# Moving the tensor engine's wait for the score banks, in the slot that carries the feed-forward part, from the first key to the first up-projection

## What is computed

```python
x = x + block(layernorm(x), cond, ctx)      # h1 = adaln(x); x += mha(h1, h1)
                                            # h2 = adaln(x); x += mha(h2, context)
                                            # h3 = adaln(x); x += glu_ff(h3)
x = x + moe(layernorm(x))                   # 8 experts, 2 of them per token
# mha: 16 heads of 64; scores / sqrt(64); softmax; weighted values; output projection
# glu_ff: u = x @ w1 + b1; (a * gelu(gate)) @ w2 + b2, width 512
```

## Time and profile before

| | |
|---|---|
| median of three runs | 2303.79 us |
| lowest, highest | 2301.26, 2304.38 us |
| the profiled execution | 2302.38 us |
| its span in the trace | 2300.6 us |
| tensor engine busy | 2129.9 us (93%) |
| vector, scalar, GpSimd engine busy | 1265.9, 1282.2, 821.0 us |
| mean granted clock of the tensor engine | 0.972 of 2.4 GHz |

### The profile page before, as it was taken

One profiled execution on the slowest core, in us unless ns is written; L12 is line 12 of the kernel. 1 busy time (PEld: TensorE's weight loads), 2 busy tenths in 40 slices (PEclk: granted clock), 3 DMA queues, 4 the chain that ended last, 5 costly groups with the idle time before them and its releaser, 6 DMA issues. The chain is left out here.

```text
span 2300.6 us, 36836 instructions
## 1 busy us (share of the span) xinstructions
PE 2129.9 (93%) x10284; PEld 1293.0 (56%) x10285; DVE 1265.9 (55%) x3230; ACT 1282.2 (56%) x2450; POOL 821.0 (36%) x1022
## 2 busy tenths in 40 slices
PE   4899999999999999999999999999998777799996
PEld 4455555555555555555555555555555455577774
DVE  3454656565656666565656565656454434245454
ACT  3565666665666666656666666666556433344432
POOL 1132223334242424233333333332423333355553
PEclk8999999999999999999999999999999978999998
DMA  4001111111121111111211111111122111122264
GB/s 141 24 24 42 46 32 47 47 47 50 41 56 41 47 51 41 46 52 40 55 42 46 42 46 42 50 42 46 51 61 84 47 38 39 33 57 57 59 216 151
DMA packets 134421, 127.63 MB, mean 55 GB/s; under 512 B 14649, under 2 KB 108377, under 8 KB 134298
## 3 DMA queue, kind: packets, MB, share of 16 engines
q1 hardware_dynamic: 125018, 108.03, 16.9%
q0 software_dynamic: 9280, 18.28, 2.4%
HBM read 86.63 MB, written 40.67 MB: 55 GB/s over the span
## 5 line engine op out<-in xcount | busy, mean ns | idle before, releaser
L1651 POOL TENSOR_TENSOR pr<-pr,sm 128x512 f32<-128x512 f32 x256 | 262.7, 1045 | 760.4 <-DVE sm L1255 760.4
L706 PE MATMUL ps<-tt,V 128*128 128x512 f32 x1024 | 501.7, 594 | 4.5 <-ACT tt L981 4.5
L981 ACT ACTIVATE kp<-ps 128x512 f32<-128x512 f32 x512 | 295.8, 600 | 198.7 <-PE ps L269 195.3
L1245 DVE TENSOR_REDUCE mx<-ps 128x8 f32<-128x512 f32 x256 | 176.7, 690 | 335.5 <-PE ps L663 332.3
L663 PE MATMUL ps<-kp,hf 128*64 128x256 f32 x2048 | 279.2, 395 | 11.6 <-DVE pr L1248 8.7
L269 PE MATMUL ps<-hk,M 128*128 128x512 f32 x768 | 250.6, 450 | 27.2 <-DVE pr L1248 25.1
L981 ACT ACTIVATE tt<-ps 128x512 f32<-128x512 f32 x512 | 273.6, 587 | 2.2 <-PE ps L693 2.2
L269 PE MATMUL ps<-cT,M 128*128 128x512 f32 x768 | 268.5, 473 | 0.0
L663 PEld LDWEIGHTS ps<-kp,hf 128*64 128x64 f32 x2048 | 125.4, 137 | 202.6 <-DVE pr L1248 130.2
L981 ACT ACTIVATE pt<-ps 128x512 f32<-128x512 f32 x256 | 153.5, 599 | 151.9 <-PE ps L675 151.9
L1009 ACT ACTIVATE pr<-pr 128x512 f32<-128x512 f32 x256 | 161.6, 631 | 136.3 <-DVE pr L1248 134.7
(11 more groups left out here) (221 smaller groups left out, 3199.1 us busy)
## 6 DMA issues: line engine op xcount, KB each, us to landing
mod<-emb_s SPq DMA_DIRECT2D x96, 256.0 KB, 4.3
xr<-rows_s SPq DMA_DIRECT2D x144, 66.0 KB, 1.8
cb<-y_s SPq DMA_DIRECT2D x32, 256.0 KB, 2.8
x_in<-in_x_dram SPq DMA_DIRECT2D x16, 256.0 KB, 4.3
xn_s<-x_in SPq DMA_DIRECT2D x16, 256.0 KB, 2.0
res<-xn_s SPq DMA_DIRECT2D x16, 256.0 KB, 2.7
c_in<-in_ctx_dram SPq DMA_DIRECT2D x16, 256.0 KB, 4.7
y_s<-res SPq DMA_DIRECT2D x16, 256.0 KB, 2.0
```

Of the source, the lines that this page charges most:

```text
L706: mm = nc.tensor.matmul(psO[:], Vw[a][:, g * HG + head_at(h), :], tt[:, h, :], start=(g == 0 and h == 0), stop=(g == 1 and h == HG - 1))
L981: return nc.scalar.activation(o, i, ACT.Copy)
L1245: nc.vector.tensor_reduce(mx[:, p % 2, :], heads(psS[p % 2][:]), AX_X, ALU.max).then_inc(max_done, 1)
L1651: tensor(v, v, sm[:, p, :].unsqueeze(2).broadcast_to([P, HG, 64]), ALU.mult).then_inc(prob_done, 1)
```

## The change

In slot u = 3 with a feed-forward part (`glu_here`, from round 2 on), the tensor engine waited for `sub_done` of its four score tiles ahead of key 0. Now it waits for the same value at h = 1, directly ahead of the first `glu_up` of the slot, behind keys 0 and 1 and behind `place`.

```diff
                 glu_here = u == 3 and ok(i - 2)
-                if glu_here and here:
-                    pe.wait_ge(sub_done, 4 * seq(i, u) + 4)
                 stages = STAGES[u]
...
                     if glu_here and h in (1, 3, 5):
+                        if here and h == 1:
+                            pe.wait_ge(sub_done, 4 * seq(i, u) + 4)
                         glu_up(i - 2, h // 2 + 1)
```

## The result

| | before | changed |
|---|---|---|
| median of nine runs, us | 2302.65 | 2308.38 |
| lowest, highest, us | 2299.14, 2304.84 | 2301.97, 2312.35 |
| ratio, 95% interval | | 1.0029, 1.0019 to 1.0039 |
| the profiled execution, us | 2302.38 | 2310.75 |
| its span, us | 2300.6 | 2309.0 |

Forecast was no measurable change, at 2304.1 us in 2300.0 to 2309.0. The median lies in that range, but the change is slower by 5.7 us, beyond the 0.2% that I had set.

The account below looks back on a forecast made before the run. The tensor engine, busy 2129.9 of 2300.6 us, was taken as the bound. Terms 0 - 0.48 + 0.35 + 0.44 = +0.31 us, added to a median of 2303.79, gave 2304.1 us, range 2300.0 to 2309.0.

Parts of the forecast that it names:

- Rounds 3 to 14, gain 0: Twelve rounds with keys and `place`: the 2.08 us idle slides behind the keys, `place` still waiting for `tt` copies; gain 0.
- Round 2, -0.48 us: Round without `place`: keys start earlier, the whole 0.48 us idle goes and the up-projection starts earlier; -0.48 us.
- Rounds 15 and 16, gain 0: Rounds without keys: the wait already merged with that of `place` for the `tt` copies, 3.8 and 3.6 us; gain 0.
- The wait in its new place, +0.35 us: Between `place` and up-projection: always met, but its 32 ns register operation is no longer covered in eleven loop rounds; +0.35 us.
- The clock behind the idle, +0.44 us: Two of twelve rounds still at 1.2 GHz, now slowing `place` and up-projection at 1.62 us each, against 2.80 before; +0.44 us.
- my slower rival: 1.2 GHz behind the slid idle in more than two rounds, deciding from five; all twelve would give 2320.3 us; chance 0.12.

Follow-up runs that it names:

- e14: The changed kernel run a third time with nothing altered; ratio 1.0027 to the kernel before.
- e3: The changed kernel with eight unread matmuls of 512 columns filling the idle ahead of `place`; ratio 0.9996 to the kernel before.
- e6: The kernel before with eight unread matmuls of 512 columns filling its idle ahead of key 0; ratio 0.9981 to the unfilled kernel before.
- e1: The changed kernel with the up-projection moved ahead of `place`, both still held until the `tt` copies of tile 3; ratio 1.0005 to the kernel before.
- e13: The changed kernel with eight matmuls of 32 columns in the idle ahead of `place`; ratio 1.0001 to the kernel before.
- e2: The kernel before with two more 32-column matmuls between the idle and key 0 in the twelve rounds that place a chunk; ratio 1.0018.
- e8: The `sub_done` wait put behind key 0, ahead of key 1, splitting the idle in two; ratio 1.0024 to the kernel before.
- e4: The changed kernel with the up-projection ahead of `place` in all rounds, waiting for the subtraction alone; ratio 0.9871 to the kernel before.
- e12: The changed kernel with four unread matmuls of 512 columns in the idle ahead of `place`; ratio 0.9991 to the kernel before.

## Why the prediction was wrong

- *Rounds 3 to 14, gain 0.* Right, to a hundredth: `place` 1.76 us behind the subtraction against 1.77, full periods of 108.92 us in both. The idle slid behind the keys, as forecast. It is 2.01 us there, not 2.08.
- *Round 2, -0.48 us.* Right in kind. `weigh` to up-projection was 3.12 us (285.49 to 288.61) and is 2.56:

```profile
286.53 1.13 PE L693 MATMUL ps<-pt,c_tm 64*128 64x512 f32 x4
287.59 1.66 PE L269 MATMUL ps<-hk,M 128*128 128x512 f32 x6
289.09 1.55 PE L269 MATMUL ps<-h,W 128*128 128x512 f32 x6
```

- *Rounds 15 and 16, gain 0.* The wait of round 15 is 3.73 us, it was 3.77. That of round 16 came out at 2.2 us instead of 3.6, and at 3.6 in e14. Low stretches fall in these rounds in both kernels, at other points, and no run takes this term apart from them.
- *The wait in its new place, +0.35 us.* It was nothing: 0.46 or 0.47 us from `place` to up-projection, before and after, in every full round. So neither the wait nor its register operation added anything that can be measured. The 50 to 100 ns that the Trainium skill ("Advanced Engine Details and Errata", Network/Comms) gives for the reading of a semaphore do not show in this trace.
- *The clock behind the idle, +0.44 us.* This is the step that failed, in the words "The idle is as long as before and the work around it is the same, so I keep the count". The price of one was nearly right (1.62 us forecast, 1.55 measured for a short stretch), but in part by luck: I had counted 0.40 us of it between `place` and the up-projection, where a short stretch costs nothing (0.46 us, as at full clock); the up-projection and the key behind it lost it instead. `place` itself ran at 1.2 GHz only in the two long ones, and there that part was right (0.87 and 2.70 us, 835.98 to 839.55), and as much again came behind it. The count was not: six rounds instead of two, and two of them long at 3.10 us, a size that I hadn't thought of. Instead of 2 x 1.62 = 3.2 us it was 12.4 in the traced execution, against 2.7 before. By the medians the change lost 5.7 us, so the typical execution probably has fewer or shorter ones. The work around the idle is *not* the same: full-size keys stood behind it, and now it is `place`. The mechanism is the one of my slower rival, whose point of decision (five rounds) was passed. It had 0.12, too little: the trace of before already had a case in which `place` stood directly behind an idle, in round 15, and there it ran at 1.2 GHz, though that idle was 3.77 us long. I took the price from that row and not the hint about the count.

So in the traced executions the time that the change cost in rounds 3 to 14 is shown to be the clock (full periods of 108.92 us in both; e3, e6). That what stands behind the idle matters is supported by e1, whose trace with an up-projection there has half as many low rounds and no long one, and by the long stretches, which came with `place` directly behind the fall; it is one trace of e1, and its time does not settle it. Why `place` there makes it worse is open. That small matmuls count fully as idle is hard to hold after e13. That 1.2 GHz lasts 6.8 us was seen in these rounds only where small matmuls stood right behind an idle of 2 us (seven times in the three traces of the change, once in e2), and not in e8, where `place` stood behind an idle of 0.75 us. How many of the low rounds come from the place of the idle in time, round after round, and how many from what stands behind it, no run separates. I have no rule that gives all of these.

## What to carry to other kernels

Before moving a wait, look for the next wait in program order and follow both to their source: where both hang on one instruction, moving one lets the idle slide and wins nothing; bringing forward work that hangs on less, as the up-projection in e4, wins. When an idle on the tensor engine slides, look at what will stand directly behind it and at its granted clock, round by round, because the same idle can cost four times as much there (12.4 us against 2.7 in the traces here). Where an idle of 2 us can't be removed, four to eight matmuls with no reader took all low rounds away (e12, e3, e6); faster than the kernel before beyond the interval was e6 alone, by 0.19%.

## What I had not expected of the hardware

- The same idle of 2.0 us was followed by 1.2 GHz in two of twelve rounds in one place and in six or seven in another, and the counts came out alike in the other executions that were traced, though not always in the same rounds.
- A low stretch lasted either some 3.4 or some 6.8 us (1.55 or 3.10 us of time lost), though the engine was busy for 6.52 of 6.70 us in the long one.
- Adding 88 matmuls of 512 columns to the eleven periods made them 12.4 us shorter in the changed kernel.
